# The out-attention's chain of layer 1, moved half a step back in the pair loop of a four-layer graph stack

## What is computed

```python
def _gat_heads(x, adj, W, a):
    Wh = jnp.einsum('bnf,hfo->bhno', x, W)
    f1 = jnp.einsum('bhno,ho->bhn', Wh, a[:, :O])
    f2 = jnp.einsum('bhno,ho->bhn', Wh, a[:, O:])
    e = f1[:, :, :, None] + f2[:, :, None, :]
    e = jnp.where(e > 0, e, LEAKY_ALPHA * e)
    e = jnp.where(adj[None, None] > 0, e, NEG_INF)
    attn = jax.nn.softmax(e, axis=-1)
    return jnp.einsum('bhnm,bhmo->bhno', attn, Wh)

h = jax.nn.elu(_gat_heads(enc_inputs, adj, W_heads, a_heads))       # four heads
h = jnp.transpose(h, (0, 2, 1, 3)).reshape(B, N, -1)
out = jax.nn.elu(_gat_heads(h, adj, W_out[None], a_out[None])[:, 0]) # the out-attention
ffn = jnp.maximum(out @ w1 + b1, 0.0) @ w2 + b2
```

## Time and profile before

| | us |
|---|---|
| median of three runs | 3117.1 (3115.95 to 3119.1) |
| the profiled execution's own time | 3117.14 |
| its span in the trace | 3115.4 |
| TensorE busy | 3003.0 (96%) |
| VectorE busy | 2262.0 (73%) |
| GpSimd busy | 2070.8 (66%) |
| ScalarE busy | 1737.4 (56%) |

### The profile page before, as it was taken

One profiled execution on the slowest core, in us unless ns is written; L12 is line 12 of the kernel. 1 busy time (PEld: TensorE's weight loads), 2 busy tenths in 40 slices (PEclk: granted clock), 3 DMA queues, 4 the chain that ended last, 5 costly groups with the idle time before them and its releaser, 6 DMA issues.

```text
span 3115.4 us, 65262 instructions
## 1 busy us (share of the span) xinstructions
PE 3003.0 (96%) x19324; PEld 2656.3 (85%) x19324; DVE 2262.0 (73%) x4877; ACT 1737.4 (56%) x4250; POOL 2070.8 (66%) x2901
## 2 busy tenths in 40 slices
PE   8999989999999999999999999999799999999997
PEld 6878879888888888888888888889688888888885
DVE  7777656767676676766767667674788888888885
ACT  3333345555555555555555555553566767676675
POOL 5666656666666666666666656641588888888885
PEclk9999999999999999999999999999999999999999
DMA  6555421111111111111111111111633332333320
GB/s 200 179 187 183 148 83 34 49 51 47 44 48 49 47 47 44 53 45 47 47 44 54 44 47 47 45 50 55 193 96 95 101 93 87 99 101 99 93 74 31
DMA packets 308643, 247.65 MB, mean 79 GB/s; under 512 B 150060, under 2 KB 215644, under 8 KB 308316
## 3 DMA queue, kind: packets, MB, share of 16 engines
q1 hardware_dynamic: 296796, 221.64, 23.9%
q10 hardware_dynamic: 9216, 16.78, 1.4%
q0 software_dynamic: 2560, 8.39, 0.8%
HBM read 162.83 MB, written 83.91 MB: 79 GB/s over the span
## 4 chain that ended last, share of the span: by engine, by line
PE 65%; POOL 8%; issue 7%; DMA 2%; SPq 1%; DVE 1%; ACT 1%; POOLq 0%; DVEq 0%; ACTq 0%
PE wop L2026 18%; PE hp L2012 16%; PE wop L47 9%; PE hp L2145 5%; PE hp L47 5%; POOL w_first L1300 3%; PE agg L1992 2%; PE agg_b L1992 2%; DMA att_scratch<-who 2%; PE agg_b L2034 2%; PE agg_b L2112 2%; PE agg L2112 2%; SPq L1181 1%; POOL who L1305 1%; POOL g_terms L1365 1%
## 5 line engine op out<-in xcount | busy, mean ns | idle before, releaser
L1300 POOL TENSOR_TENSOR w_first<-xd,v_row 128x512 f32<-128x512 f32 x480 | 637.8, 1344 | 88.2 <-ACT w_first L1436 88.2
L2012 PE MATMUL hp<-yT_hi,big_hi 128*128 128x256 f32 x2048 | 589.8, 288 | 0.0
L2012 PE MATMUL hp<-yT_lo,big_hi 128*128 128x256 f32 x2048 | 579.3, 283 | 0.0
L2012 PE MATMUL hp<-yT_hi,big_lo 128*128 128x256 f32 x2048 | 579.0, 283 | 0.0
L1729 DVE TENSOR_TENSOR hT_lo<-ex,hT_hi 128x512 fp32r<-128x512 f32 x256 | 269.8, 1054 | 229.8 <-ACT hT_hi L1458 229.7
L2026 PE MATMUL wop<-big_hi,hT_hi 128*128 128x512 f32 x1024 | 408.3, 399 | 0.0
L2026 PE MATMUL wop<-big_lo,hT_hi 128*128 128x512 f32 x1024 | 399.9, 391 | 0.0
L2026 PE MATMUL wop<-big_hi,hT_lo 128*128 128x512 f32 x1024 | 399.9, 391 | 0.0
L2012 PEld LDWEIGHTS hp<-yT_lo,big_hi 128*128 128x128 f32 x2048 | 392.8, 192 | 0.0
L2012 PEld LDWEIGHTS hp<-yT_hi,big_hi 128*128 128x128 f32 x2048 | 392.3, 192 | 0.2
L2012 PEld LDWEIGHTS hp<-yT_hi,big_lo 128*128 128x128 f32 x2048 | 392.2, 192 | 0.0
(11 more groups left out here) (219 smaller groups left out, 7969.9 us busy)
## 6 DMA issues: line engine op xcount, KB each, us to landing
x0f<-in_x_turned SPq DMA_DIRECT2D x64, 256.0 KB, 2.7
xt<-in_x SPq DMA_DIRECT2D x64, 256.0 KB, 2.9
x_scratch<-w_first ACTq DMA_DIRECT2D x64, 256.0 KB, 2.3
xa<-x_scratch SPq DMA_DIRECT2D x64, 256.0 KB, 2.7
att_hi_scratch<-att_hi SPq DMA_DIRECT2D x64, 256.0 KB, 2.0
att_lo_scratch<-who SPq DMA_DIRECT2D x64, 256.0 KB, 2.0
att_hi<-att_hi_scratch SPq DMA_DIRECT2D x64, 256.0 KB, 3.6
att_lo<-att_lo_scratch SPq DMA_DIRECT2D x64, 256.0 KB, 4.4
```

The source lines that it names most:

```text
L1300: nc.gpsimd.tensor_tensor(terms[:, k % TR, :], xd[:], v_row[:, k, :], ALU.mult).then_inc(terms_ready, 1)
L2012: ins = nc.tensor.matmul(hp[half][:, s * 2 * P:(s + 1) * 2 * P], a, b, start=c == 0 and i == 0, stop=c == KC - 1 and i == 2)
```

## The change

Within a step, work of the out-attention is moved on all four computing engines; no instruction of the loop is added or taken away, and no DMA changes place. On TensorE the scores of tile 2m go behind `out_part(p, 0, *)`, its turn behind `project(p, 2, 1)`, the scores of 2m+1 into the middle of `out_part(p, 1, *)`, the sums of 2m behind it, and the turn of 2m+1 between the halves of `project(p, 3)`. The turn of the head attention's tile 2p+3 goes ahead of `out_part(p, 1, *)`. Three waits move with them: `ao_.summed` of 2m, `at.turned_ready` (now for both tiles of the pair), and `att_ready` of 2m, now asked for in `aggregate(p+1, 0)` and ahead of the last sums.

```diff
@@ GpSimd, step
                     if fresh(p + 2):
-                        products_of(*first, range(4, 6))
-                    if pair(m):
-                        ao_.pool_prob(nc, pool, 2 * m)
-                    if fresh(p + 2):
-                        products_of(*first, range(6, NV))
+                        products_of(*first, range(4, NV))
                     if pair(p + 2):
                         at.pool_diag(nc, pool, 2 * p + 4, p + 2, 0, i64)
-                    if pair(m):
-                        ao_.pool_diag(nc, pool, 2 * m + 1, i64)
                     if pair(p + 1):
                         at.pool_prob(nc, pool, 2 * p + 3)
+                    if pair(m):
+                        ao_.pool_prob(nc, pool, 2 * m)
+                        ao_.pool_diag(nc, pool, 2 * m + 1, i64)
                     if fresh(p + 2):
-                        products_of(*second, range(0, 2))
+                        products_of(*second, range(0, 4))
                     if pair(m):
                         ao_.pool_prob(nc, pool, 2 * m + 1)
...
@@ ScalarE, step
                     if fresh(p + 2):
-                        dots(*first, (1, 2))
+                        dots(*first, (1,))
                     if pair(m):
                         keep_wo(m, 0)
                     h_hi(k, 1)
                     if pair(m):
                         keep_wo(m, 1)
                     if fresh(p + 2):
-                        dots(*first, (3,))
+                        dots(*first, (2, 3))
                     exp(k + 1, 0)
                     if fresh(p + 2):
                         dots(*first, (4,))
-                    if pair(m):
-                        ao_.act_exp(nc, act, 2 * m)
                     exp(k + 1, 1)
...
-                    if pair(m):
-                        ao_.act_turned(nc, act, 2 * m)
                     if fresh(p + 2):
                         dots(*first, (7,))
+                    if pair(m):
+                        ao_.act_exp(nc, act, 2 * m)
                     exp(k + 2, 0)
-                    if pair(m):
-                        ao_.act_exp(nc, act, 2 * m + 1)
                     if fresh(p + 2):
                         dots(*second, (0,))
                     exp(k + 2, 1)
-                    if pair(m):
-                        out_exp(2 * m)
+                    if pair(p + 1):
+                        at.act_turned(nc, act, 2 * p + 3, p + 1, 1, agg_done)
+                    if pair(m):
+                        ao_.act_turned(nc, act, 2 * m)
...
                     h_hi(k + 2, 0)
                     if pair(m):
+                        ao_.act_exp(nc, act, 2 * m + 1)
+                    if fresh(p + 2):
+                        dots(*second, (2,))
+                    h_hi(k + 2, 1)
+                    if pair(m):
+                        out_exp(2 * m)
+                    if fresh(p + 2):
+                        dots(*second, (3,))
+                    exp(k + 3, 0)
+                    if pair(m):
+                        ao_.act_turned(nc, act, 2 * m + 1)
                         split_att(2 * m, 0, m + 1)
...
@@ VectorE, step
                     h_lo(k, 1)
-                    if pair(m):
-                        ao_.dve_before_exp(nc, dve, 2 * m, fill1)
                     elu(k + 1, 0)
                     if pair(p + 1):
                         at.dve_peak(nc, dve, 2 * p + 3, fill1)
-                    if pair(m):
-                        ao_.dve_after_exp(nc, dve, 2 * m)
                     elu(k + 1, 1)
                     for n in range(4):
                         y_lo(p, 1, n)
                     h_lo(k + 1, 0)
-                    if pair(m):
-                        out_f(2 * m + 1, 1)
                     if pair(p + 1):
                         at.dve_after_exp(nc, dve, 2 * p + 3)
                     h_lo(k + 1, 1)
+                    if pair(m):
+                        ao_.dve_before_exp(nc, dve, 2 * m, fill1)
+                        out_f(2 * m + 1, 1)
+                        ao_.dve_after_exp(nc, dve, 2 * m)
                     elu(k + 2, 0)
+                    elu(k + 2, 1)
                     if pair(m):
                         ao_.dve_before_exp(nc, dve, 2 * m + 1, fill1)
-                    elu(k + 2, 1)
+                    h_lo(k + 2, 0)
                     if pair(m):
                         ao_.dve_after_exp(nc, dve, 2 * m + 1)
+                    h_lo(k + 2, 1)
+                    if pair(m):
                         out_elu(2 * m)
...
@@ TensorE, step
                     project(p, 1, 0)
-                    if pair(m):
-                        pe.wait_ge(at.summed, capped(2 * p + 4, T))
-                        ao_.pe_scores(nc, pe, 2 * m, same_graph)
                     project(p, 1, 1)
...
                     if pair(m):
+                        ao_.pe_scores(nc, pe, 2 * m, same_graph)
+                    project(p, 2, 0)
+                    project(p, 2, 1)
+                    if pair(p + 1):
+                        at.pe_turn(nc, pe, 2 * p + 3, ident)
+                    if pair(m):
+                        pe.wait_ge(ao_.summed, 2 * m + 1)
                         ao_.pe_turn(nc, pe, 2 * m, ident)
-                    project(p, 2, 0)
+                    out_part(p, 1, 0)
+                    out_part(p, 1, 1)
                     if pair(m):
                         pe.wait_ge(ao_.turned_ready, 2 * (2 * m + 1))
                         ao_.pe_scores(nc, pe, 2 * m + 1, same_graph)
-                    project(p, 2, 1)
-                    if pair(m):
-                        pe.wait_ge(at.turned_ready, capped(2 * (2 * p + 3), 2 * T))
+                    out_part(p, 1, 2)
+                    out_part(p, 1, 3)
+                    if pair(m):
+                        pe.wait_ge(at.turned_ready, capped(2 * (2 * p + 4), 2 * T))
                         out_sums(2 * m, 0)
-                    for c in range(KC):
-                        out_part(p, 1, c)
+                    project(p, 3, 0)
                     if pair(m):
                         pe.wait_ge(ao_.summed, 2 * m + 2)
                         ao_.pe_turn(nc, pe, 2 * m + 1, ident)
...
```

More of the change, by code:

```diff
@@ L1333, in step @@
                     if fresh(p + 2):
-                        products_of(*first, range(4, 6))
+                        products_of(*first, range(4, NV))
+                    if pair(p + 2):
+                        at.pool_diag(nc, pool, 2 * p + 4, p + 2, 0, i64)
+                    if pair(p + 1):
+                        at.pool_prob(nc, pool, 2 * p + 3)
                     if pair(m):
                         ao_.pool_prob(nc, pool, 2 * m)
+                        ao_.pool_diag(nc, pool, 2 * m + 1, i64)
                     if fresh(p + 2):
-                        products_of(*first, range(6, NV))
-                    if pair(p + 2):
-                        at.pool_diag(nc, pool, 2 * p + 4, p + 2, 0, i64)
-                    if pair(m):
-                        ao_.pool_diag(nc, pool, 2 * m + 1, i64)
-                    if pair(p + 1):
-                        at.pool_prob(nc, pool, 2 * p + 3)
-                    if fresh(p + 2):
-                        products_of(*second, range(0, 2))
+                        products_of(*second, range(0, 4))
                     if pair(m):
@@ L1349, in step @@
                     if fresh(p + 2):
-                        products_of(*second, range(2, 5))
+                        products_of(*second, range(4, 6))
                     if pair(m):
@@ L1353, in step @@
                     if fresh(p + 2):
-                        products_of(*second, range(5, NV))
+                        products_of(*second, range(6, NV))
                 at.pool_diag(nc, pool, 2, 1, 0, i64)
@@ L1539, in step @@
                     if pair(m):
+                        ao_.act_exp(nc, act, 2 * m + 1)
[9 more added lines that the diff above has]
+                        ao_.act_turned(nc, act, 2 * m + 1)
                         split_att(2 * m, 0, m + 1)
                     if fresh(p + 2):
[L1542 to L1545, removed]
-                    if pair(m):
[L1547 to L1552, removed]
+                        dots(*second, (4, 5))
                     exp(k + 3, 1)
@@ L1805, in step @@
                     h_lo(k + 1, 1)
+                    if pair(m):
+                        ao_.dve_before_exp(nc, dve, 2 * m, fill1)
+                        out_f(2 * m + 1, 1)
+                        ao_.dve_after_exp(nc, dve, 2 * m)
                     elu(k + 2, 0)
+                    elu(k + 2, 1)
                     if pair(m):
                         ao_.dve_before_exp(nc, dve, 2 * m + 1, fill1)
-                    elu(k + 2, 1)
+                    h_lo(k + 2, 0)
                     if pair(m):
                         ao_.dve_after_exp(nc, dve, 2 * m + 1)
+                    h_lo(k + 2, 1)
+                    if pair(m):
                         out_elu(2 * m)
```

(4 more changed lines are left out.)

## The result

| | before | after |
|---|---|---|
| median, us | 3117.6 | 3079.6 |
| span of the profiled execution, us | 3115.4 | 3078.7 |
| one pass of the pair loop, us | 55.45 | 54.06 |

The ratio is 0.9877, with a 95% interval of 0.986 to 0.9894: the changed kernel is 38 us faster. The median before, 3117.6 us, is of four runs; the prediction knew three of them (3117.1 us). The time lies inside the stated range, near its slow end. The forecast of 3062 us took 55 us off; 38 came.

What follows compares the result with a forecast made beforehand. The prediction took TensorE's work plus its idle time to bound the pair loop. From 3117.1 us, minus 62.4 for waits removed, plus 7.0 for a new one, it forecast 3061.7 us (stated as 3062), range 3053 to 3084 us.

Steps and rivals of the forecast that it cites:

- The two waits that go: TensorE ahead of the scores of 2m and 2m+1: 1.21 and 1.02 us a pass vanish, 62.4 us in all.
- The new wait: TensorE at scores of 2m+1, for ScalarE's read of 2m's turned block: 0.25 us a pass, 7.0 us in 28.
- the two legs: From the end of out_part(p,0) to scores of 2m+1: TensorE's work 9.87 us, the out-attention's chain 10.12 us.
- yT_lo and banks_free: At the head attention's turn after out_part(p,0): VectorE's yT_lo keeps about 0.6 us of cover.
- Its own signs: Right: pass about 53.5 us, L101 once with 0.1 to 0.5 us. Wrong: waits at L148 or L268, L101 over 1.
- (a): At scores of 2m+1 the chain slips through without a new wait: 3054.7 us; chance 0.24.
- (b): At scores of 2m+1, a stretched row product or later GpSimd product: wait about 1.4 us a pass, 3094 us; chance 0.13.
- (c): At scores of 2m+1, the high end: wait 2.25 us a pass, gain eaten, 3118 us; chance 0.05.
- (d): At scores of 2m+1, high end plus another half product: wait 2.9 us a pass, slower, 3136 us; chance 0.05.

Runs made afterwards that it cites:

- e3: The changed kernel with scores of 2m+1 behind three quarters of out_part(p,1) and VectorE's dve_peak behind yT_lo: 3050.9 us.
- b2: The kernel before with one GpSimd move, ao_diag of 2m+1 ahead of the head attention's diag: 3085.3 us.
- e1: The changed kernel with scores of 2m+1 behind three quarters of out_part(p,1) instead of half: 3058.6 us.
- e4: The changed kernel with dot 0 of the second tile moved on ScalarE behind exp(k+2,1) and the two reads of turned blocks: 3057.5 us.
- e2: The changed kernel with VectorE's dve_peak of tile 2p+3 behind the four yT_lo, its exp behind dots 5 and 6: 3070.3 us.
- e7: The changed kernel with one part undone, dot 2 of the first tile ahead of keep_wo again on ScalarE: 3089.2 us.
- e6: The changed kernel with dot 0 of the second tile behind the reads of turned blocks and dve_peak behind yT_lo: 3050.9 us.
- b1: The kernel before with one ScalarE move, dot 2 behind keep_wo: 3107.4 us.
- e5: The changed kernel with GpSimd's sixteen products a pass over 256 of 512 columns, so its output differs: 3052.5 us.

## Why the prediction was right, and where it was off

**The two waits that go.** Right in place and cause. Both went whole, in all 28 passes. Their size was a little low: before minus 53.07 (e3) is 2.39 us a pass, 66.8 us, not 2.23 and 62.4 us. The 0.16 us between them fits the 0.1 us or so that a wait cost beyond its distance (b2: 1.10 us a pass for 1.02). One reason given beside them does not hold: the steps outside the loop are not free of dot products. Step p = 1 has them (from 484.28 us on in the trace of before) and still did not wait.

**The new wait.** Its place, its releaser and the two legs were right; e1 and e4 take it away from either side. Its size was 0.59 us, not 0.25. Counted from the turn at 1957.20, TensorE's leg was 1966.98 - 1957.20 = 9.78 us (forecast 9.87), the other 1967.57 - 1957.20 = 10.37 us (10.12). The nearly right sum hides errors that cancel. ScalarE and VectorE of the changed kernel, start us and length:

```profile
1958.07 0.61 ACT L1455 CAST hT_hi<-ex 128x512 fp32r<-128x512 f32 x1
...
1960.52 0.35 ACT L127 ACTIVATE ao_ex<-ao_e,ao_peak 128x64 f32<-128x64 f32 x1 [0.43 <-DVE ao_peak L120]
...
1965.20 0.63 ACT L1433 ACTIVATE w_first<-w_first 128x512 f32<-128x512 f32 x1 [3.62 <-POOL w_first L1300]
...
1967.08 0.44 ACT L158 COPY ao_turned<-agg_b 64x64 f32<-64x64 f32 x2
```

```profile
1958.71 0.77 DVE L1725 TENSOR_TENSOR hT_lo<-ex,hT_hi 128x512 fp32r<-128x512 f32 x1 [0.42 <-ACT hT_hi L1455]
...
1959.65 0.25 DVE L113 SCALAR_TENSOR_TENSOR ao_e<-ao_e 128x64 f32<-128x64 f32 x1
...
1960.76 0.73 DVE L1739 CUSTOM_DVE_ANT_0 att_hi<-who,ao_row 128x512 f32<-128x512 f32 x1 [0.28 <-issue]
...
1961.53 0.98 DVE L1743 CUSTOM_DVE_ANT_0 att_hi<-who,ao_row 128x512 f32<-128x512 f32 x1
...
1962.44 0.15 DVE L133 RECIPROCAL ao_inv<-ao_total 128x1 f32<-128x1 f32 x1
```

hT_hi began 0.87 us behind the turn, not 0.2, because dots 5 and 6 were still ahead of it, themselves behind a late yT_hi. hT_lo took 0.77 instead of 1.25, and the step to the exp 0.87 instead of 1.25: both missed the meeting I had charged them with. The row products and the queue paid instead: from the exp to the reciprocal 1.92 us passed, not 1.45, and prob of 2m began 0.36 us behind the reciprocal's end. The claim that GpSimd has nothing to do while VectorE makes them was wrong. Its prob of the head attention ran until 1962.99, and prob of 2m stood behind it:

```profile
1960.90 2.09 POOL L260 TENSOR_TENSOR ah_prob<-w_first,ah_inv 128x256 f32<-128x256 f32 x2
1962.95 0.73 POOL L140 TENSOR_TENSOR ao_prob<-ao_ex,ao_inv 128x64 f32<-128x64 f32 x2
```

The term was forecast too small by more than half: with what a wait costs beyond its distance it costs 0.71 us a pass (e1), 19.9 us, where 7.0 stood in the sum.

**yT_lo and banks_free.** This step of the prediction failed, though the time came out inside the range. I gave it 0.6 us of cover or more; it lost 0.21 us a pass, 0.29 by the pass (e2), some 8 us. The reasoning was that VectorE loses 2 us of work ahead of yT_lo and gets who sooner. Both are so, but the time did not arrive:

```profile
1944.51 1.64 DVE L1739 CUSTOM_DVE_ANT_0 att_hi<-who,ao_row 128x512 f32<-128x512 f32 x1 [0.29 <-ACT who L1463]
...
1947.56 1.50 DVE L1725 TENSOR_TENSOR hT_lo<-ex,hT_hi 128x512 fp32r<-128x512 f32 x1
1948.98 1.50 DVE L1716 TENSOR_SCALAR ex<-ex 128x512 f32<-128x512 f32 x1
...
1956.45 0.69 DVE L1708 TENSOR_TENSOR yT_lo<-agg_b,yT_hi 128x512 fp32r<-128x512 f32 x1
```

Each of the first three met a product of GpSimd. In the kernel before, the same steps were these:

```profile
1982.24 1.49 DVE L1729 TENSOR_TENSOR hT_lo<-ex,hT_hi 128x512 fp32r<-128x512 f32 x1
...
1985.46 0.42 DVE L1720 TENSOR_SCALAR ex<-ex 128x512 f32<-128x512 f32 x1
```

hT_lo met a product there too, so it is not what changed. The row products took 0.69 us each there, because GpSimd sat idle for ao_f while they ran. The earlier copy of `who` took this quiet time away. That alone did not make yT_lo late, though: e7 gives the quiet time back, and yT_lo comes later still. The early copy, even with its meeting, won more than it lost. What ate the 2 us of lighter work is mainly the first elu step, which I had not charged with meetings at all: 1.50 instead of 0.42 us in this place, and a mean of 0.79 us instead of 0.49, 76 us of VectorE's time in the whole execution. yT_lo ended at 1957.14 and the turn began at 1957.20.

**The sum again.** 66.8 - 19.9 - 8.1 = 38.8 us in the loop. All three terms are differences between passes of these runs, so that they add up proves nothing further. Outside the loop, the unrolled step p = 0 became 3.0 us longer (from its first aggregation to that of p = 1, 45.5 us before, 48.5 after). Of this 1.3 us are the wait for yT_lo (1.2 in the list of waits), 0.6 us a wait for VectorE's ex, and 0.85 us the first projection, which ran 6.77 us before and 7.62 after, at a mean granted clock of 0.83 and 0.72. TensorE came out of a wait of some 9 us in both; why the clock rose later in the changed kernel stays open (stretch, length, busy times with PE first, granted clock):

```profile
425.24:432.01 6.77, 6.77 (x50) 6.77 (x50) 3.74 (x10) 1.64 (x4) 4.28 (x6) 0.83 0.29 84
```

```profile
424.46:432.08 7.62, 7.62 (x50) 7.62 (x50) 3.21 (x7) 0.92 (x2) 3.98 (x5) 0.72 0.18 44
```

The prediction had no term for p = 0. With 0.3 us won in the other unrolled steps and the 0.8 and 0.6 us ahead of and behind the loop, the spans' difference of 36.7 us is accounted for to 0.4 us.

**Its own signs.** L101 in the list once a pass with 0.4 us, put down to ao_turned, came as forecast. The pass of about 53.5 us did not (54.06), and the loss at L268 is one of the signs that it had called wrong.

**The rivals.** (a) needed what e3 and e6 gave it by further moves; even then it ends at 3051, not at 3055. (b) lay 14 us on the other side of the result, and what came is a mixture: the mechanism of the forecast with meetings as in (b), in another step. (c) and (d) did not come; product 7 was indeed late, since dot 5 stood behind yT_hi, but prob of 2m was pushed by 0.4 us and not by two products.

## What to carry over

When waits on an in-order engine are removed by moving a chain, write down every foreign instruction that then stands in it on the other queues; one dot product in ScalarE's order, with the product that it waits for, was worth 22 us here (e4). Try the smallest move that answers each wait first: two one-line moves in the old order (3076 us) gave what the rearrangement gave, and the rearrangement was worth it only once its own two new waits were taken out (3051 us). Idle time of an engine that is not the bound can still be worth something, if another engine's long steps run undisturbed in it: in b1 the copy came over 1 us sooner and the scores gained 0.35 us. Count the unrolled first and last steps of a loop as well; p = 0 alone took back 3 us here.

## What the runs showed of the hardware

That VectorE and GpSimd stretch each other was expected; that it reaches the one-input elu step over SBUF was not: the same instruction of 128x512 took 0.42 us alone and 1.50 us beside a product, and its mean followed the length of GpSimd's products (0.79 us in the changed kernel, and 0.56 us in e5 with half of it; 0.49 us in the kernel before, where the step rarely met one). The Trainium skill (SBUF — State Buffer, "SBUF: two separate sides") says that a VectorE instruction in a mode with two ports takes the shared pair as well, and that whichever engine starts first holds it for its whole instruction. The trace agrees: 1.50 us is no more than the 0.42 us alone and one whole product of 1.29 us together. That the elu step runs in such a mode no run here shows. Elu's second step, which reads PSUM and SBUF, kept its mean of 0.69 us in all these kernels.

A wait of TensorE cost 0.1 us more than the distance it showed: 0.71 for 0.59 us (e1), 0.29 for 0.21 us (e2). e7 made one wait 0.37 us longer and the pass 0.36 us, so the extra came once for a wait and did not grow with it. Why it arises stays open.
